# A routing sort whose one-hots are made column by column in 16 bits and carry only the token code, with the expert weights multiplied in the last adds

## The reference, cut to what matters

```python
top_vals, top_idx = jax.lax.top_k(logits, 2)          # 2 of 8 experts per token
w = jax.nn.softmax(top_vals, axis=-1)
w_full = jnp.einsum('bsk,bske->bse', w, jax.nn.one_hot(top_idx, 8, dtype=w.dtype))
for e in range(8):
    h = jax.nn.gelu(jnp.einsum('bsd,dh->bsh', xn, W1[e]) + b1[e], approximate=False)
    y_e = jnp.einsum('bsh,hd->bsd', h, W2[e]) + b2[e]
    y = y + y_e * w_full[..., e, None]
```

## Time and profile before

| | |
|---|---|
| median of 3 runs | 6197.29 us (6196.83 to 6203.05) |
| the profiled execution's own time | 6198.35 us |
| its span | 6196.6 us |
| mean granted TensorE clock | 0.841 |
| PE busy | 4354.5 us (70%) |
| DVE busy | 3632.5 us (59%) |
| POOL busy | 4050.3 us (65%) |
| ACT busy | 1291.3 us (21%) |

### The profile page before, as it was taken

How to read it: one execution, slowest core, us unless ns; L and a number is a source line. 1 busy time by engine, 2 the same in 40 slices (tenths; PEclk the granted TensorE clock), 3 DMA queues, 4 the chain that set the end, 5 groups by cost and what they waited for, 6 DMA issues and landing times.

```text
span 6196.6 us, 63953 instructions
## 1 busy us (share of the span) xinstructions
PE 4354.5 (70%) x16894; PEld 2841.8 (46%) x16895; DVE 3632.5 (59%) x10972; ACT 1291.3 (21%) x3391; POOL 4050.3 (65%) x4182
## 2 busy tenths in 40 slices
PE   4899799999957777675466565645565555647995
PEld 1555455555534444443244444424433333545663
DVE  7887788888846666665555555544444444443223
ACT  0587455555500000000100000000000000212442
POOL 2777777777757777777577777767777776003442
PEclk8999899999968888997777877777787776757997
DMA  3400333333353333334444444473333335200114
GB/s 116 126 1 1 85 104 104 103 103 103 104 127 112 112 112 111 112 112 94 131 137 139 136 137 138 128 191 109 105 105 105 105 105 98 90 27 29 61 62 158
DMA packets 331514, 641.97 MB, mean 104 GB/s; under 512 B 82320, under 2 KB 201700, under 8 KB 330704
## 3 DMA queue, kind: packets, MB, share of 16 engines
q0 software_dynamic: 191808, 490.67, 29.4%
q1 hardware_dynamic: 131652, 139.90, 6.9%
q10 hardware_dynamic: 7756, 7.97, 0.4%
HBM read 551.23 MB, written 87.01 MB: 103 GB/s over the span
## 4 chain that ended last, share of the span: by engine, by line
PE 46%; DVE 14%; issue 13%; POOL 8%; DMA 8%; ACT 1%; DVEq 1%; ACTq 0%; SPq 0%; POOLq 0%; PEldq 0%
PE PS L1367 27%; POOL gbuf L538 8%; DVE acc L946 7%; DMA gbuf<-table,idx 7%; PE PS L1335 6%; PE PS L1544 3%; PE PS L1567 3%; PE PS L1397 2%; DVE ohg L955 2%; PE PS L1524 1%; PE PS L1560 1%; PE PS L1435 1%; DMA gbuf<-ye_d 1%; PE PS L1492 1%; DVE gbuf L1194 0%
## 5 line engine op out<-in xcount | busy, mean ns | idle before, releaser
L538 POOL DMA_INDIRECT gbuf<-table,idx x3520 | 3364.4, 956 | 1184.1 <-issue 810.6
L1367 PE MATMUL PS<-gbuf,ohg 128*128 128x257 f32 (+1 forms) x7040 | 2273.6, 469 | 1383.0 <-issue 760.4
L1367 PEld LDWEIGHTS PS<-gbuf,ohg 128*128 128x128 f32 x7040 | 1539.5, 231 | 2108.3 <-issue 1323.4
L946 DVE TENSOR_TENSOR acc<-acc,PS 128x257 f32 (+1 forms) x3520 | 1492.8, 424 | 1715.2 <-PE PS L1367 1692.8
L955 DVE TENSOR_SCALAR ohg<-iota,dl 128x128 f32<-128x128 f16 x2640 | 813.7, 315 | 86.4 <-issue 86.4
L1335 PE MATMUL PS<-region 128*128 128x440 f16 x3328 | 687.3, 349 | 0.0
L546 POOL DMA_INDIRECT scattered_d<-acc x384 | 373.7, 973 | 127.1 <-issue 121.0
L1335 PEld LDWEIGHTS PS<-region 128*128 128x128 f16 x3328 | 324.5, 97 | 282.7 <-issue 1.6
L640 ACT ACTIVATE region<-region,acc 128x128 f16<-128x128 f16 x832 | 334.0, 401 | 522.6 <-DVE region L897 516.3
L896 DVE TENSOR_SCALAR region<-iota_c,acc 128x880 f16<-128x880 f16 x832 | 411.0, 494 | 23.2 <-issue 23.2
L1335 PE MATMUL PS<-acc,region 128*128 128x440 f16 x1792 | 335.3, 350 | 7.7 <-ACT region L641 7.7
(11 more groups left out here) (284 smaller groups left out, 3570.6 us busy)
## 6 DMA issues: line engine op xcount, KB each, us to landing
gbuf<-table,idx POOLq DMA_INDIRECT x3520, 2.8
table<-acc SPq DMA_DIRECT2D x21, 896.0 KB, 6.7
region<-xt_d SPq DMA_DIRECT2D x98, 128.0 KB, 2.2
gbuf<-ye_d SPq DMA_DIRECT2D x12, 1024.0 KB, 7.6
xpad_d<-acc SPq DMA_DIRECT2D x1, 6272.0 KB, 22.0
xn_d<-acc SPq DMA_DIRECT2D x49, 128.0 KB
xt_d<-acc SPq DMA_DIRECT2D x49, 128.0 KB
table<-acc SPq DMA_DIRECT2D x49, 128.0 KB
```

Source lines behind the costliest of these rows:

```text
L538: gp.indirect_dma_start(gbuf[:, c % U, 0:F], None, tables[p], bass.IndirectOffsetOnAxis(idx[p % 2][:, c:c + 1], 0)).then_inc(s_g[c % U // ...
L946: TT(a, a, chunk_sum(p, k), ALU.add).then_inc(s_acc[p], 1)
L1367: m = MM(chunk_sum(p, k), ohg[:, k, :], gbuf[:, k, 0:width(p)], start=True, stop=True)
```

## The change

Of the sort: `ohc` and the weight half of `ohv` are gone, and so is POOL's product. For each of the 98 columns DVE makes `ohs` from the 16-bit iota with one `tensor_scalar`, and `ohv` with another one that compares with the chunk and multiplies by the code in the same instruction. Both outputs are 16-bit floats. The code is the integer token code plus 1024, whose 16 bits are read as a float, so two casts are added ahead of the sort (`code16`, `val`) and three instructions behind it (`v16`, `vi` and the subtraction of 1024). The loops are written out; the buffers hold 14 columns, so DVE may be two groups of `ES` = 7 columns ahead of PE. PE multiplies 16-bit tiles with 108 moving columns where it had 32-bit tiles with 216.

Of the experts: ACT's product by `wgt` and its semaphore `s_scl` are gone, and POOL's scatter waits on `s_b2`, which DVE's bias add counts. In the last stage DVE does, for each block and choice, one `scalar_tensor_tensor` of 128x256 that multiplies by `wt` and adds: eight instructions for a group where there were two. SP waits for `s_ge` once before it starts the last stage's loads.

```diff
-        fc = carve(gbuf_flat, {"ohs": ((CE7, P), f32), "ohc": ((CE7, NCE), f32), "ohv": ((CE7, 2, NCE), f32)})
+        fc = carve(gbuf_flat, {"ohs": ((RING, P), f16), "ohv": ((RING, NCE), f16)})
...
-            gp.iota(fb_["val"], pattern=[[1, 2], [2 * P, NB]], base=1, channel_multiplier=2,
-                    allow_small_or_imprecise_dtypes=True).then_inc(s_ei, 1)
-            with pool.Fori(0, NK // CE7) as i:
-                pool.wait_ge(s_eoh, i + 1)
-                for f, v in enumerate((fb_["val"], fb_["wt"].rearrange("p j b -> p (j b)"))):
-                    if f == 0:
-                        gp.tensor_tensor(fc["ohv"][:, :, 0, :], fc["ohc"], v[:, ds(i * CE7, CE7)].unsqueeze(2).broadcast_to([P, CE7, NCE]), ALU.mult).then_inc(s_eohv, 1)
+            gp.iota(fb_["code"], pattern=[[1, 2], [2 * P, NB]], base=1 + LOWEST, channel_multiplier=2).then_inc(s_ei, 1)
...
-                    pool.wait_ge(s_scl, i * ER + (k + 1))
+                    pool.wait_ge(s_b2, i * ER + (k + 3))
...
-                    act.wait_ge(s_b2, i * ER + (k + 3))
-                    A(fe["y"][:, k, :], fe["y"][:, k, :], ACT.Copy, scale=sm["wgt"][:, ds(i * ER + k, 1)]).then_inc(s_scl, 1)
...
+            link(V.tensor_copy(fb_["code16"], fb_["code"]))
+            link(V.tensor_copy(fb_["val"], fb_["code16"].bitcast(f16)))
             dve.wait_ge(s_xfree, 2 + NG + 1)
-            with dve.Fori(0, NK // CE7) as i:
-                dve.wait_ge(s_eused, i + 1)
-                c = ds(i * CE7, CE7)
-
-                def wide(v, n):
-                    return v[:, c].unsqueeze(2).broadcast_to([P, CE7, n])
-                TT(fc["ohc"], iota_c[:, 0:NCE].unsqueeze(1).broadcast_to([P, CE7, NCE]), wide(fb_["chunk"], NCE), ALU.is_equal).then_inc(s_eoh, 1)
-                TT(fc["ohs"], iota_f[:, :].unsqueeze(1).broadcast_to([P, CE7, P]), wide(fb_["slot"], P), ALU.is_equal)
-                dve.wait_ge(s_eoh, i + 1)
-                TT(fc["ohv"][:, :, 1, :], fc["ohc"], wide(wt.rearrange("p j b -> p (j b)"), NCE), ALU.mult).then_inc(s_eopen, 1)
+            for c in range(NK):
+                if c >= 2 * ES and c % ES == 0:
+                    dve.wait_ge(s_eused, c // ES - 1)
+                at = c % (2 * ES)
+                TS(fc["ohs"][:, at, :], iota_h[:, :], fb_["slot"][:, c:c + 1], None, ALU.is_equal)
+                m = TS(fc["ohv"][:, at, :], iota_c[:, 0:NCE], fb_["chunk"][:, c:c + 1], fb_["val"][:, c:c + 1],
+                       ALU.is_equal, ALU.mult)
+                if c % ES == ES - 1:
+                    m.then_inc(s_eoh, 1)
...
-            v = PS[:, 0, 0:NCE]
+            v = fd["v"]
+            link(V.tensor_copy(fd["v16"], PS[:, 1, 0:NCE]))
+            link(V.tensor_copy(fd["vi"], fd["v16"].bitcast(u16)))
+            link(TS(v, fd["vi"], float(-LOWEST), 0.0, ALU.add, ALU.max))
...
-            link(V.tensor_copy(sm["wgt"], PS[:, 0, NCE:2 * NCE]))
...
-                x2 = accs[1][0:m, q * G:q * G + n, 0:F]
-                link(TT(x2, x2, yl[q % 2][0:m, 0:n, 0, :], ALU.add))
-                TT(x2, x2, yl[q % 2][0:m, 0:n, 1, :], ALU.add).then_inc(s_add, 1)
+                for j in range(2):
+                    for b in range(n):
+                        x2 = accs[1][0:m, q * G + b, 0:F]
+                        a = STT(out=x2, in0=yl[q % 2][0:m, b, j, :], scalar=wt[0:m, j, q * G + b:q * G + b + 1], in1=x2,
+                                op0=ALU.mult, op1=ALU.add)
+                    if j == 0:
+                        link(a)
+                a.then_inc(s_add, 1)
```

More of the change, by code:

```diff
@@ L106, in gps_layer @@
     NCE = -(-((2 * N + NE * (P - 1)) // P) // ER) * ER
-    CE7 = 7
+    ES = 7
+    LOWEST = 1024
     NG = NB // G
-    assert U // IB == ER and OH % IB == 0
+    assert U // IB == ER and OH % IB == 0 and 2 * NB * P + LOWEST < 31744 and 2 * NB % ES == 0 and 2 * ES <= RING
     assert NB % R7 == 0 and NB == NG * G + 1 and NG % 2 == 0 and SORT_TURNS % 2 == 0 and HC <= 512
@@ L300, in gps_layer @@
         (s_gt, s_gtc, s_u, s_z, s_v1, s_d1, s_fold, s_shift, s_xf, s_xfd, s_xfree, s_xft, s_xftc, s_lg, s_lgc,
-         s_ei, s_ed, s_ex, s_ecnt, s_etot, s_eoh, s_eohv, s_eused, s_eopen, s_esort, s_iw, s_ready,
-         s_it, s_t1e, s_c1, s_up, s_b1, s_ge, s_t2, s_c2, s_dn, s_b2, s_scl, s_yfreed, s_add, s_od) = [sem(n) for n in (
+         s_ei, s_ed, s_ex, s_ecnt, s_etot, s_eoh, s_eused, s_esort, s_iw, s_ready,
+         s_it, s_t1e, s_c1, s_up, s_b1, s_ge, s_t2, s_c2, s_dn, s_b2, s_yfreed, s_add, s_od) = [sem(n) for n in (
              "s_gt s_gtc s_u s_z s_v1 s_d1 s_fold s_shift s_xf s_xfd s_xfree s_xft s_xftc s_lg s_lgc "
-             "s_ei s_ed s_ex s_ecnt s_etot s_eoh s_eohv s_eused s_eopen s_esort s_iw s_ready "
-             "s_it s_t1e s_c1 s_up s_b1 s_ge s_t2 s_c2 s_dn s_b2 s_scl s_yfreed s_add s_od").split()]
+             "s_ei s_ed s_ex s_ecnt s_etot s_eoh s_eused s_esort s_iw s_ready "
+             "s_it s_t1e s_c1 s_up s_b1 s_ge s_t2 s_c2 s_dn s_b2 s_yfreed s_add s_od").split()]
         s_fl = [sem(f"s_fl{n}") for n in range(2)]
@@ L467, in _ @@
                 sp.wait_ge(s_g[k], XG0 + 16 * (NCE // ER + 1))
+            sp.wait_ge(s_ge, NCE + 1)
             for q in range(NG + 1):
@@ L1516, in _ @@
             MM(PS[:, 0, 64:64 + NE], ones[:, :], fb_["cnt"], start=True, stop=True).then_inc(s_etot, 1)
-            pe.sem_inc(s_eused, 1)
-            pe.wait_ge(s_eoh, 1)
-            MM(PS[:, 0, 0:2 * NCE], z16[:, :], iota_c[:, 0:2 * NCE], start=True, stop=False)
-            with pe.Fori(0, NK // CE7) as i:
-                pe.wait_ge(s_eopen, i + 1)
-                pe.wait_ge(s_eohv, i + 1)
-                for k in range(CE7):
-                    m = MM(PS[:, 0, 0:2 * NCE], fc["ohs"][:, k, :], fc["ohv"][:, k, :, :].rearrange("p f c -> p (f c)"),
-                           start=False, stop=False)
-                m.then_inc(s_eused, 1)
-            MM(PS[:, 0, 0:2 * NCE], z16[:, :], iota_c[:, 0:2 * NCE], start=False, stop=True).then_inc(s_esort, 1)
+            MM(PS[:, 1, 0:NCE], z16[:, :], iota_c[:, 0:NCE], start=True, stop=False)
+            for c in range(NK):
+                if c % ES == 0:
+                    pe.wait_ge(s_eoh, c // ES + 1)
+                m = MM(PS[:, 1, 0:NCE], fc["ohs"][:, c % (2 * ES), :], fc["ohv"][:, c % (2 * ES), :], start=False, stop=False)
+                if c % ES == ES - 1:
+                    m.then_inc(s_eused, 1)
+            MM(PS[:, 1, 0:NCE], z16[:, :], iota_c[:, 0:NCE], start=False, stop=True).then_inc(s_esort, 1)
             def load_experts(ap):
```

9 lines of the change are left out of this document (5 added, 4 removed).

## The result

The changed kernel takes **6107.02 us** (median of 4 runs, 6103.21 to 6110.24) where the kernel before took 6200.07 us beside it (4 runs): ratio 0.985, 95% interval 0.9833 to 0.9867. The forecast was 6104 us, the range 6098 to 6119. The profiled execution has a span of 6101.5 us, 95.1 us under that of before; it is the fastest of the four. By the medians the gain is 6200.07 - 6107.02 = 93.05 us, for which the forecast had 93.0.

What follows compares the result with a forecast made beforehand. The sort, 131.0 us with engines taking turns, was taken as the removable part of the path. Terms -96.9 (sort), +0.5 (unpacking), -0.65 (loop end) and +4 (last stage) summed to -93.0 us: 6104 us, range 6098 to 6119.

Steps and rivals of the forecast that it cites:

- So 98 x 0.32 = 31.4 us: Sort: DVE takes 0.16 us for each of two one-hots in all 98 columns, 31.4 us together.
- rival A: Sort: new DVE instructions cost over 0.16 us: 6109, 6113 or, without overlap (last form), 6120 us; chance 20%, last form 4%.
- The pause of 0.8 us: Sort: DVE's 196 instructions meet one pause with nothing to wait for, +0.8 us.
- PE's end: Sort: after DVE, PE still does the last seven columns, at most 1.3 us, 1.7 with signal and closing matmul.
- rival B: Sort: PE at half clock becomes the bound at 0.38 us a column, +6 us, 6110; chance 4%.
- Casts, unpacking, loop end: Two casts and entry ahead of the sort +0.2 us, unpacking behind it +0.5, end of the expert loop -0.65.
- PE is the bound with 99% busy and does not wait for either; nothing is gained in 108 chunks: Expert loop: dropping ACT's product and scattering earlier gains 0 us, as PE is busy 449.8 of 455.6 us.
- +4 us: Last stage: longer adds, 0.9 us a group, lie on up to six buffer rounds of load and adds; 0 to 5.4 us.
- rival C: Last stage: the longer adds hide behind the transfers, 88% busy, giving 6100 us; chance 9%.
- The clock at the loop's start: Start of the expert loop: 2 us allowed in the forecast's own range for the clock's rise.
- Rival D: Expert loop: PE's clock stays at the 1.2 GHz level; in all 108 chunks +420 us, 6525, slower than before; chance 2%.
- the own range: Whole kernel: likeliest case's range, 6100 to 6109 us, from the last stage, the pause and the clock's rise.

Runs made afterwards that it cites:

- experiments 1 and 2: 1: kernel before with only the weights' part, 6194.41 us; 2: changed kernel with ACT's product by ones back in place, 6110.23, or behind the `hT` copy, 6107.72.
- w_only: Kernel before with only the change's second part (no ACT product, scaled last adds), old sort kept: 6194.41 us against 6201.27, ratio 0.9991.
- tt_last: Changed kernel with two adds of 1024 columns a group back in the last stage, weights left out: 7285.34 us on a chip where the kernel before took 7381.85.
- four_buffers: Changed kernel with four buffers instead of two for the last stage's loads: 7262.63 us on another chip, ratio 0.9843 to the kernel before.
- dve_kinds: Changed kernel with 152 unused DVE instructions of eleven kinds behind the sort: spacing 0.097 us with no pointer scalar, 0.159 with one, 0.219 with two.

## Why the prediction came out as it did

The stages were read rightly and the change acts mainly where it was said to, in the sort. That the total came out within 3 us is luck all the same: two terms were too favourable (by 4.5 and 2.8 us), and two gains were missing (7.4 and 2.0).

- **"So 98 x 0.32 = 31.4 us"** is the term that was too small: DVE took 0.38 a column, 37.4 us, 6.0 more. The pause that did not come (0.8) and a shorter end on PE (0.7) made 4.5 of it. It was the first form of rival A ("with 0.05 for the second pointer: +4.9 us"), which was given 20% with its other forms. The earlier trace rows had the price, 1.28 against 1.23, and the prediction set it aside because the second operation "lies in the same pass". That is true, the second operation is free; but a pointer is not part of the operation and has a price of its own, 0.061 us.
- **Overlap of the instructions.** Of rival A the last form (each starts when the one before has ended) is refuted: 0.38 a column, not 0.25 + 0.30 = 0.55. The Trainium skill, "VectorE: DVE Perf Modes", section "The DRAIN you can't avoid", has the next instruction start only with an empty pipe, but adds in the same paragraph that "A next op that is not held starts earlier", which the prediction left out. The trace agrees with that addition: `ohv` starts 0.17 us after an `ohs` that lasts 0.25.
- **The pause of 0.8 us** did not come: DVE was busy for 37.38 us from the first of the 196 instructions to the last. The Trainium skill, "Runtime: NRT & Kernel Launch", section "Instruction fetch mechanics", has fetching mostly hidden; for these 196 instructions the trace agrees with it and not with the row that I took.
- **PE's end**: 5553.00 - 5552.04 = 1.0 us instead of 1.7; a group of seven takes 0.81, not 1.3. No wait on `s_eused`, as said; rival B is out although the clock was at its lower level of 1.2 GHz (0.50) throughout.
- **Casts, unpacking, loop end**: +0.2, +0.5 and -0.65, all as worked out.
- **"PE is the bound with 99% busy and does not wait for either; nothing is gained in 108 chunks"** is the step that was wrong. The 1% that was left were 5.8 us of the 455.6, on the path, at the end of every turn of four chunks, and ACT's product was their cause by way of PE's sequencer (experiments 1 and 2). The loop got 7.4 us shorter, 9.5 in `w_only`. That is more than the 5.8 us of idle time: PE's busy time fell too, from 449.8 to 447.8 us for the same products, so the 99% counted some waiting as work.
- **The last stage, "+4 us"**: right in mechanism (load and adds in turn through two buffers), 4.7 by the means of three and seven runs; rival C (hidden, 6100) is out. The single execution showed 6.8.
- **The clock at the loop's start**: the 2 us kept for it came out as -2.0. The first up product to the first down product took 7.1 us here, but 7.6 in `tt_last` and 9.9 in `four_buffers`, whose instructions are the same up to there: the first ones take anything from 3.62 us, as at the lower level of the clock, to the 1.88 of the loop at the higher, and which gets which differs from run to run. So this -2.0 can't be put down to the change. Rival D did not come: granted clock 1.00 in the loop.
- **The sums.** The terms named for the own range, if the 2 us of the clock go both ways, give 6097 to 6107 and not 6100 to 6109; the measured median of 6107.02 lies in both, towards their upper ends. The 9.69 us that the earlier trace rows gave for a turn of the old sort are those of its first turn; the mean is 130.98 / 14 = 9.36. The forecast does not use it.
- **What stays open**: a turn of the changed kernel has one chunk of 4.26 us where the other three take 4.16, and `w_only` and `dve_kinds` have none such. Over 27 turns these 0.10 us are 2.7 us, about what the loop's gain of 7.4 lacks against the 9.5 of `w_only`. The trace puts it down to a register load of DVE at its own turn's end. `dve_kinds` differs from the changed kernel in that engine's instructions ahead of the loop only, so it may hang on where the loop lies in DVE's list; that is not shown, and why was not tried.

## What to carry to other kernels

Where small vector instructions set the pace, count their pointer scalars and not their operations: fuse the second operation, but let an idle engine take a second pointer. A loop in which an engine is 99% busy still has a gain in it if the last 1% comes at each turn's end: look at when the engine's sequencer reaches the branch, and what keeps its last semaphore wait from passing early. And where a load and its use alternate through two buffers, the longer use is paid once a round (here 4.7 of the 5.4 us of six rounds), while two more buffers pay back far more than it cost.

## What the runs showed of the hardware

- A pointer scalar costs VectorE 0.061 us per instruction, in both forms measured (16-bit compares of 108 columns, 32-bit adds of 256); a constant and a second operation cost nothing. Independent instructions overlap: 0.097 us apart while each lasts 0.18.
- A register load by TensorE's sequencer takes 1.23 to 1.47 us in the four turn ends shown. It is hidden if the branch lies 0.56 us ahead of the start of the turn's last product; if the branch comes with that start it costs 0.27 us, and 0.2 us behind it 0.40.
- With four buffers the loads of 1 MB land later each (10.4 us median instead of 7.2) and the stage is shorter all the same (56.9 instead of 74.2 us), with the transfers busy 99% instead of 80%.
